# Second self-attention of a decoder: the output product moved to the head of each step, the token normalisation moved to GpSimd

## The reference

```python
h = NUM_HEADS                                  # 16 heads of 64
q = _split_heads(x @ Wq + bq, h)               # x: the normalised tokens
k = _split_heads(x @ Wk + bk, h)
v = _split_heads(x @ Wv + bv, h)
scale = 1.0 / jnp.sqrt(jnp.float32(ATTN_DIM))
pattern = jnp.einsum('bhid,bhjd->bhij', k, q) * scale
prob = jax.nn.softmax(pattern, axis=-2)
out = jnp.einsum('bhis,bhid->bhsd', prob, v)
concat = out.transpose(0, 2, 1, 3).reshape(b, s, h * dv)
return concat @ Wo + bo
```

## Time and profile before

| | |
|---|---|
| median of 3 runs | 2875.01 us (2874.33 to 2880.67) |
| profiled execution, its own time | 2879.26 us |
| span of its instructions | 2877.5 us |
| mean granted TensorE clock | 0.928 of full |
| second self-attention, first to last scores product | 1430.1 to 2168.2 us |

### The profile page before, as it was taken

How to read it: one execution, slowest core, us unless ns; L and a number is a source line. 1 busy time by engine, 2 the same in 40 slices (tenths; PEclk the granted TensorE clock), 3 DMA queues, 4 the chain that set the end, 5 groups by cost and what they waited for, 6 DMA issues and landing times. The chain is left out here.

```text
span 2877.5 us, 59452 instructions
## 1 busy us (share of the span) xinstructions
PE 2514.8 (87%) x19717; PEld 2098.5 (73%) x19717; DVE 2087.2 (73%) x4615; ACT 1446.5 (50%) x3401; POOL 1059.3 (37%) x1584
## 2 busy tenths in 40 slices
PE   7987899999758999999499999999996979996582
PEld 5875788888757999999378888888885956664231
DVE  5884898998637777776488888888875567774664
ACT  3542334334235777777265555655552456663041
POOL 3331545445301111110265555555532014333366
PEclk9988999999978999999699999999998989997586
DMA  8012000000176666664200000000002733230845
GB/s 310 0 32 88 1 1 0 0 0 0 31 292 249 220 220 220 220 219 156 90 14 10 16 7 15 7 15 9 7 1 65 246 102 87 81 88 11 267 142 168
DMA packets 156638, 266.68 MB, mean 93 GB/s; under 512 B 20944, under 2 KB 130464, under 8 KB 143200
## 3 DMA queue, kind: packets, MB, share of 16 engines
q1 hardware_dynamic: 140400, 215.91, 22.1%
q0 software_dynamic: 11168, 31.21, 3.7%
q10 hardware_dynamic: 4944, 17.96, 1.6%
HBM read 191.85 MB, written 73.17 MB: 92 GB/s over the span
## 5 line engine op out<-in xcount | busy, mean ns | idle before, releaser
L1723 ACT ACTIVATE a_prob<-a_s_ps,a_ntop 128x256 f32<-128x256 f32 x512 | 235.6, 473 | 304.3 <-DVE a_ntop L1808 304.3
L1776 POOL TENSOR_TENSOR a_prob<-a_prob,a_rden 128x1024 f32<-128x1024 f32 x128 | 242.5, 1895 | 302.4 <-DVE a_rden L1813 302.4
L3204 POOL DMA_INDIRECT e0x_xg<-token_rows,e_order x78 | 75.3, 965 | 384.7 <-PE e0x_t_ps L3251 342.5
L2411 ACT ACTIVATE x1a_prob<-x1a_st_ps,x1a_mask_now 128x512 f32<-128x512 f32 x256 | 162.2, 686 | 92.0 <-PE x1a_st_ps L2330 90.6
L1301 ACT ACTIVATE x0b_sq<-x0b_f 128x1024 f32<-128x1024 f32 x64 | 67.9, 1060 | 274.2 <-DVE x0b_f L1375 274.1
L2486 DVE TENSOR_REDUCE x1a_top<-x1a_s_ps 128x4 f32<-128x1024 f32 x128 | 154.9, 1222 | 66.9 <-PE x1a_s_ps L2314 65.0
L1808 DVE TENSOR_REDUCE a_ntop<-a_s_ps 128x4 f32<-128x1024 f32 x128 | 156.2, 1221 | 38.9 <-PE a_s_ps L1646 38.8
L68 PE MATMUL e0x_up_ps<-e0x_xT_high,e0x_up_w_high 128*128 128x256 f32 x624 | 180.4, 289 | 1.1 <-DVE e0x_up_w_low L3331 1.1
L68 PE MATMUL e0x_up_ps<-e0x_xT_high,e0x_up_w_low 128*128 128x256 f32 x624 | 177.5, 285 | 0.0
L68 PE MATMUL e0x_up_ps<-e0x_xT_low,e0x_up_w_high 128*128 128x256 f32 x624 | 177.3, 284 | 0.0
L68 PE MATMUL e0x_y_ps<-e0x_down_w_high,e0x_hT_high 128*128 128x256 f32 x624 | 176.6, 283 | 0.0
(11 more groups left out here) (648 smaller groups left out, 8708.1 us busy)
## 6 DMA issues: line engine op xcount, KB each, us to landing
e0x_up_raw<-up_rows SPq DMA_DIRECT2D x39, 1024.0 KB, 4.8
e0x_down_raw<-down_rows SPq DMA_DIRECT2D x39, 1024.0 KB
x_qk<-head_rows SPq DMA_DIRECT2D x384, 64.0 KB
head_rows<-x1p_rows_out SPq DMA_DIRECT2D x32, 512.0 KB, 3.8
e1w_ew<-in_L_ffn_expert_w_dram SPq DMA_DIRECT2D x8, 2048.0 KB
sorted_tokens<-zeros SPq DMA_DIRECT2D x10, 1024.0 KB, 19.6
sorted_results<-e0x_y SPq DMA_DIRECT2D x39, 256.0 KB
down_rows<-e0w_downT ACTq DMA_DIRECT2D x8, 1024.0 KB, 7.3
```

The lines of the kernel that those rows point to most:

```text
L1723: last = act.activation(prob[:, h % RING, n, t, :], s_ps[:, n, t * SEQ:(t + 1) * SEQ], ACT.Exp, bias=ntop[:, h % RING, n, t:t + 1], accum_ ...
L1776: last = pool.tensor_tensor(p, p, scale_of, ALU.mult)
L2411: last = act.activation(prob[:, c % 2, j, 2 * (h % 2):2 * (h % 2) + 2, :], st_ps[:, :, j * SEQ:(j + 1) * SEQ], ACT.Exp, bias=mask_now[:, p ...
```

## The change

In each step TensorE issues first `attend`, then the turns, then the scores, then the side products; before it was scores, turns, side products, `attend`. No lag and no wait is changed. The token normalisation of the next batch goes from VectorE, at the end of step h = 2, to GpSimd, at h = 3 behind the normalisation of a pair's probabilities; that of batch 0 goes to GpSimd too. The spacer in the first experts' stage has 37 columns for 26.

```diff
@@ -1700,15 +1700,15 @@
                     for h in range(PAIRS):
                         turning, attending = lagging(b, h, TURN), lagging(b, h, ATTEND)
                         pieces = [p for p in pieces_of(h) if live(b + p[3])]
-                        if live(b):
-                            scores(b, h)
+                        if attending:
+                            attend(*attending)
                         if turning:
                             turn(*turning, 0)
                             turn(*turning, 1)
+                        if live(b):
+                            scores(b, h)
                         for i, kind, number, ahead in pieces:
                             piece(i, kind, number, b + ahead, b, q)
-                        if attending:
-                            attend(*attending)
@@ -1776,11 +1776,22 @@
+                def tokens(b):
+                    for t in range(TPB):
+                        tile = TPB * b + t
+                        ins = pool.tensor_scalar(xn[:, t, :], sh.x[:, tile, :], sh.stats[:, tile, 0:1], sh.rstd[:, tile:tile + 1],
+                                                 ALU.subtract, ALU.mult)
+                    ins.then_inc(s_xn, 1)
+
                 def batch(b, q):
                     for h in range(PAIRS):
                         own = lagging(b, h, 1)
                         if own:
                             normalise(*own)
+                        if h == 3 and live(b) and live(b + 1):
+                            pool.wait_ge(filled["X"], per_batch["X"] * (b + 1))
+                            pool.wait_ge(combine.s_rstd, b + 2)
+                            tokens(b + 1)
@@ -1792,17 +1803,12 @@
+                tokens(0)
                 for b in range(-1, BATCH + 1):
                     batch(b, b % 2)
 
             @block.vector
             def _(dve):
-                def normalise(b):
-                    for t in range(TPB):
-                        ins = dve.tensor_scalar(xn[:, t, :], sh.x[:, TPB * b + t, :], sh.stats[:, TPB * b + t, 0:1],
-                                                sh.rstd[:, bass.ds(TPB * b + t, 1)], ALU.subtract, ALU.mult)
-                    ins.then_inc(s_xn, 1)
-
@@ -1879,12 +1885,7 @@
-                        if h == 2 and live(b) and live(b + 1):
-                            dve.wait_ge(filled["X"], per_batch["X"] * (b + 1))
-                            dve.wait_ge(combine.s_rstd, b + 2)
-                            normalise(b + 1)
-
-                normalise(0)
+
                 over_batches(dve, batch)
@@ -3166,7 +3167,7 @@
         UNROLLED = 5
-        LOOP_PLACE = 26
+        LOOP_PLACE = 37
```

## The result

The changed kernel takes 3061.15 us (median of three runs, 3055.83 to 3070.42) against 2875.01: a ratio of 1.0652, 95% interval 1.0629 to 1.0674, 186.1 us more. The forecast was 3054, with a range of 3024 to 3068. The profiled execution is the slowest of the three; its span is 3068.5 us, 191.0 more than that of before. In the code after the change the low half of the output is L1830 (was L1824), the maximum L1814 (L1808), and VectorE's two small operations of step 3 are L3467 and L3468 (L3466 and L3467).

The account below looks back on a forecast made before the run. TensorE bound the kernel; the new order closes a ring of waits. Batch 0 +7.7, batches 1 to 13 +149.0, batch 14 +10.0, batch 15 +8.8, end +4.0, start -0.5: 2875.0 + 179 = 3054 us, range 3024 to 3068.

Parts of the forecast that it names:

- step 3: Second self-attention, step with VectorE's two small operations beside GpSimd's normalisations: 8.58 us forecast, 7.37 if VectorE is not shut out.
- The ring: Second self-attention: scores, maximum, exponents, high half, low half, `attend`, turns, next scores wait in a circle; 7.20 us a step against 5.75.
- Step 4: Step taking out pair 7, the only one ahead of the maximum, so the next `attend` doesn't wait: 5.95 us.
- A: Rival: low half is out in time, only TensorE's order costs, 0.18 to 0.22 us a step; 2899 us, chance 0.04.
- B: Rival: only the copies of the turned pairs bind, 1.1 us more in 15 batches; 2916 us, chance 0.04.
- C: Rival: faster, idle time before scores goes if the low half starts before 3.3; 2869 us at best, chance 0.02.
- D: Rival: the ring without the block in step 3, +163.3 us; 3038 us, chance 0.32.
- the block: In step 3 GpSimd's token normalisation shuts out VectorE's second small operation: 1.21 us in each of 13 batches.
- the clock: No term of its own in the sum; the range only allowed a little for it above the forecast.
- steps 7 and 0: Step 7, one side product, forecast at 7.20 us; step 0, with `mix_rows` between copies and low half, at 7.70.
- batch 0: First batch of the stage: steps 5 to 7, 13.93 us before, become 3 x 7.20, +7.7 us.
- The end: Last scores to output projection: each later `attend` needs copies of turns issued right before, 3.15 a step; 12.69 becomes 16.7, +4.0.

Follow-up runs that it names:

- experiment 5: Kernel before with the output product (`attend`) first in its step, then scores, turns, side products: 2956.62 us, ratio 1.0276.
- experiment 6: Changed kernel with ScalarE and VectorE copying every output pair at the head of the step, ahead of exponents and maximum: 2919.91 us, ratio 1.0153.
- experiment 4: Kernel before with the scores moved behind the turns only, the output product still last in its step: 2911.46 us, ratio 1.0125.
- Experiment 8: Changed kernel with the `C` product of step 7 computed twice, same operands into the same place: 3045.62 us, ratio 1.059.

## Why the prediction was right, and where it wasn't

**The ring: right, and shown.** Its 7.20 us stand in the trace link by link. It is long because of what lies in it, by experiment 5 (turns out, 1.03 less), and it exists because the low half is queued behind maximum and exponents, by experiment 6 (queue changed, 141 us back). Step 4, whose copy was already first, is 5.94 for the forecast's 5.95, the same experiment made within each batch.

**Rivals.** A, 2899 us, had its price right, 0.20 us a step by experiment 4, and its premise wrong: the low half isn't out in time. B's wait exists and is worth what is left in experiment 6, but only once the longer wait is gone. C asked for a low half before 3.3 of the step; it came at 4.59. D, the ring without the block at 3038, was right on the block.

**The term that failed: the block in step 3.** The step of the forecast "I take 1.21, since L3467 waits for its own predecessor's semaphore" is wrong. The operation, now L3468, takes 0.16 to 0.20 us. That is 13 x 1.21 = 15.7 us too many, and step 3 is 7.10 where the unblocked 7.37 was forecast, another 0.27: the low half starts 4.58 into the step, not at 4.76, since the pair's normalisation ends at 4.39 (1689.32) and not at 4.62, and TensorE's product follows it by 0.48 (1689.51 to 1689.99) and not by 0.57. Over 13 batches, three of which have 7.24, that is 3 us more. The Trainium skill (SBUF — State Buffer, "SBUF: two separate sides") lets whichever operation starts first hold the shared ports to its end. By the records GpSimd's starts 0.06 us before L3468, which by the rule would have been held some 1.2 us; either the rule or a recorded start is off by that little. No run here tells which. The row that the term was taken from is another case: L601 has one input and not two, and starts 0.83 us behind GpSimd's, well inside it. The gap of L3468 is 0.06 to 0.07 us in all 14 batches that have both, and that narrow an order was no ground for a term of 15.7.

**The term that was missing: the clock.** "A little for the clock" in the range was all. The ring made TensorE idle 2.5 us in the step with the least work, and in most batches the clock was then granted at half through turns and scores. Read from the steps 7 and 0 of batches 1 to 13, whose excess over 7.20 and 7.70 lies all in those with a clock below 1.00, it costs 12.9 us. Experiment 8 gives back 10.8 (752.44 to 741.66) by adding work, which shows the cause; in the same steps 7 it loses 2 us at a clock of 1.00, told of below. At the edges the cost is read from the trace only. In batch 0 steps 5 and 6 take 8.94 and 9.28 us at clocks of 0.74 and 0.70, 4.3 us more with step 7 than the three at 7.20; another 1.2 lie in its earlier steps, at the full clock but for the first. The end ran at 0.76 and took 5.6 us more than forecast, of which nearly 1 is not the clock's: the third of its steps, at the full clock, takes 3.47 us where 3.15 was forecast, since the low half stands behind the copies. The Trainium skill (TensorE: Matmul & The Clock Gate, "Part 1: The HAM clock gate") says that TensorE's clock is gated to 1.2 GHz when it has been little busy, and released by activity. The trace agrees, with 0.50 behind an idle stretch of 2.49 us, and so does experiment 8; why four of the 13 steps 7 kept the full clock no run here tells.

**Why the total is right all the same.** By luck in part. The ring, with what goes with it at the edges, gave 163 of the sum's 179 us. What was wrong around it cancelled: the block (-15.7) and step 3's rest (-3) stand against the clock (+12.9 in the steady batches, about +9 at the edges) and 2 us of other links at the edges. Two errors of near 20 us leave 5 in the stage, and the medians, with their scatter, differ by 7. Without the block and with the clock unforeseen, the sum would have been 3038, inside the range only. That both stayed inside is also due to a range that reached 14 us past D and past the forecast, twice the 7 us that the sum names for an error in the ring.

## What to carry to other kernels

Before moving a wait to the head of a step, follow the releaser's program order through all engines: if the work that frees the buffer is queued behind work that this very step feeds, the loop closes, and the step becomes the sum of its links, however idle every engine is. Look for the cut at the engine that is late for no reason of the data, here by copying out before starting the next maximum (141 of 186 us). This stage, when it turned from full to waiting, also lost clock: price the link operations after the longest idle stretch at the lower clock too.

## What the runs showed of the hardware that was not expected

- Adding 12 products a batch, 1.3 us of work, made the kernel 15.5 us faster, since the granted clock stayed at 1.00 where it had gone to 0.50.
- The fall is not regular. In batches 1 to 13 of the profiled execution of after, step 7 lies between 7.11 and 8.96 us and step 0 between 7.70 and 8.38.
- A two-input operation of VectorE, L3468, ran in 0.20 us beside GpSimd's token normalisation, while its neighbour on the same engine, L3467, was held to the end of GpSimd's pair normalisation (0.98 us after, 1.84 before).
- In experiment 8 four of the 13 steps 7 took 7.57 to 7.98 us at a clock of 1.00. In one, the low half starts at 1710.31, 4.59 into the step as always, and the product that it releases at 1711.67, 1.36 later instead of 0.57. What holds it for 0.8 us stays open.

```profile
1710.31 0.42 DVE L1830 TENSOR_TENSOR a_outT_low<-a_o_ps,a_outT_high 128x256 fp32r<-128x256 f32 x1 [1.08 <-ACT a_outT_high L1747]
...
1711.67 1.08 PE L1666 MATMUL a_o_ps<-a_pT,a_v 128*64 128x256 f32 x8 [1.97 <-DVE a_outT_low L1830]
```
